# PV in pairs of sequences and heads, selection by four products, and later gathers, in a one-core attention and FFN kernel

## What is computed

```python
xc = einsum('bct,bcd->bdt', x, cond_weights[subject])   # a 32x32 matrix of 32, chosen per sequence
q, k, v = rope(xc @ wq.T), rope(xc @ wk.T), xc @ wv.T   # 32 heads of 16
p = softmax(causal(q @ k.T) / 4)                        # 32x32 per head and sequence
x = x + (p @ v) @ wo.T
h = x @ W.T + 2 * lora(x)        # 8 experts of rank 16, the two best by a router
x = x + unperm(down @ gelu(up @ perm(h)))   # 16 blocks of 32 features, 128 wide inside
```

## Time and profile before

| | |
|---|---|
| median of 3 runs | 212.55 us (211.69 to 213.61) |
| the profiled execution, its own time | 214.02 us |
| its span, first to last instruction | 212.2 us |
| mean granted TensorE clock | 0.984 |
| PE busy | 203.5 us, 96% of the span |
| ACT busy | 119.2 us, 56% |
| DVE busy | 148.0 us, 70% |
| the chain that ended last | PE 89%, DVE 4%, ACT 3%, issue 1%, DMA 1% |

### The profile page before, as it was taken

How to read it: one execution, slowest core, us unless ns; L and a number is a source line. 1 busy time by engine, 2 the same in 40 slices (tenths; PEclk the granted TensorE clock), 3 DMA queues, 4 the chain that set the end, 5 groups by cost and what they waited for, 6 DMA issues and landing times.

```text
span 212.2 us, 6020 instructions
## 1 busy us (share of the span) xinstructions
PE 203.5 (96%) x2548; PEld 176.2 (83%) x2548; DVE 148.0 (70%) x287; ACT 119.2 (56%) x209; POOL 119.2 (56%) x93
## 2 busy tenths in 40 slices
PE   7799999999989999999999999999999999798993
PEld 5699987988769899986779899886698987688863
DVE  4897799999749877837619788546678995258123
ACT  2491465279763445289744454399755777533460
POOL 8263999699770203978982113969978253524000
PEclk9859999999999999999999999999999999999999
DMA  6999602005001330000062420000135200224002
GB/s 198 383 395 375 206 3 103 0 5 197 3 5 47 102 99 3 2 5 0 0 67 38 123 78 3 0 3 2 12 41 127 26 3 3 24 28 49 0 3 99
DMA packets 9930, 15.18 MB, mean 72 GB/s; under 512 B 1328, under 2 KB 5680, under 8 KB 9904
## 3 DMA queue, kind: packets, MB, share of 16 engines
q1 hardware_dynamic: 7440, 11.37, 15.6%
q0 software_dynamic: 2048, 2.88, 8.4%
q10 hardware_dynamic: 416, 0.55, 0.8%
HBM read 11.13 MB, written 3.67 MB: 70 GB/s over the span
## 4 chain that ended last, share of the span: by engine, by line
PE 89%; DVE 4%; ACT 3%; issue 1%; DMA 1%; ACTq 0%; DVEq 0%
PE ps_A L624 11%; PE ps_F L624 10%; PE ps_A L626 10%; PE ps_A L625 10%; PE ps_F L625 9%; PE ps_F L626 9%; PE ps_S L778 5%; PE ps_F L868 5%; PE ps_S L883 3%; PE ps_S L756 3%; PE ps_A L681 2%; PE ps_A L778 1%; PE ps_A L896 1%; ACT pbd L1056 1%; DMA y<-in_ids 1%
## 5 line engine op out<-in xcount | busy, mean ns | idle before, releaser
L570 POOL TENSOR_TENSOR pr<-pr,small 128x512 f32<-128x512 f32 x16 | 17.6, 1110 | 38.8 <-DVE small L1419 38.6
L1056 ACT ACTIVATE pbd<-pr 32x512 f32<-32x512 f32 x56 | 35.2, 629 | 1.3 <-DVE pr L1425 0.6
L550 POOL DMA_INDIRECT out<-y,row_at x12 | 19.8, 1647 | 11.4 <-ACT y L1056 8.9
L1117 ACT ACTIVATE pr<-pr 128x512 f32<-128x512 f32 x16 | 10.1, 633 | 24.4 <-DVE pr L1411 24.3
L507 POOL TENSOR_TENSOR rot<-rot,cst 128x512 f32<-128x512 f32 x11 | 14.4, 1305 | 15.9 <-DVE rot L1377 15.9
L1161 ACT ACTIVATE act<-ps_F 128x512 f32<-128x512 f32 x32 | 16.5, 603 | 11.3 <-PE ps_F L868 11.3
L1397 DVE TENSOR_TENSOR kbd<-kr,cst 128x512 f32<-128x512 f32 x13 | 18.9, 1486 | 3.0 <-POOL kr L511 3.0
L520 POOL TENSOR_TENSOR kbd<-kr,cst 128x512 f32<-128x512 f32 x15 | 19.4, 1320 | 0.1
L624 PE MATMUL ps_F<-x,w2T 128*128 128x256 f32 x56 | 16.1, 287 | 0.0
L626 PE MATMUL ps_F<-x,w2T 128*128 128x256 f32 x56 | 15.6, 279 | 0.0
L625 PE MATMUL ps_F<-x,w2T 128*128 128x256 f32 x56 | 15.6, 279 | 0.0
(11 more groups left out here) (237 smaller groups left out, 662.8 us busy)
## 6 DMA issues: line engine op xcount, KB each, us to landing
xt<-in_xT SPq DMA_DIRECT2D x4, 512.0 KB, 4.1
xs<-in_x SPq DMA_DIRECT2D x3, 512.0 KB, 8.0
out<-xt SPq DMA_DIRECT2D x3, 512.0 KB, 3.1
act<-in_L_attn_wk SPq DMA_DIRECT2D x1, 1024.0 KB
act<-in_L_attn_wv SPq DMA_DIRECT2D x1, 1024.0 KB
act<-in_L_attn_wo SPq DMA_DIRECT2D x1, 1024.0 KB, 7.1
xs<-in_x ACTq DMA_DIRECT2D x1, 512.0 KB, 5.1
pr<-in_L_attn_wq SPq DMA_DIRECT2D x2, 256.0 KB, 4.8
```

The lines of the kernel that those rows point to most:

```text
L550: pool.indirect_dma_start(out=out, out_offset=bass.IndirectOffsetOnAxis(ap=row_at[:, g, c:c + 1], axis=0), in_=y[:, c, :], in_offset=None, ...
L570: pool.tensor_tensor(pr[:, i, :, :], pr[:, i, :, :], mx[:, i, :].unsqueeze(2).to_broadcast([P, NH // 2, T]), ALU.mult).then_inc(normed, 1)
L1056: return sc.activation(dst, src, ACT.Copy)
```

## The change

- `vz` becomes, for each head pair, two slots (s = 0, 1, the sequences 0 and 1, or 2 and 3 of the tile) of 32 columns. Rows 0 to 63 hold the two sequences of the pair with head k = 0, rows 64 to 127 the same two with head k = 1, each with zeros in the other head's columns. `v_out` does this in 4 copies of 64 rows x 256.
- `pbd` becomes, for each head pair and s, 64 columns: two sequences' 32 tokens. Its rows are (head, sequence of the pair, key). `probs_block` does it in 8 copies of 32 rows x 256 in place of 4 of 32 x 512. The last tile's `probs_half` likewise: 4 copies for each half on VectorE and 4 on GpSimd, in place of 2 and 2.
- `pv` has still 8 products, of 64 moving columns instead of 128, and none accumulates.
- The one-hot matrix has zeros outside its own 32 rows (by `matrix_at`, which comes with the indices, and no longer waits for the constants), so 4 products with 128 rows of contraction select all, and one transpose replaces four.
- GpSimd no longer zeroes `pbd`: ScalarE copies zeros from `vz` into it (4 copies of 128 x 512), behind its `blocks(1)`. `kbd_zeros` clears half as much.
- x of group 0 is issued by SP behind the constants and ahead of `wq`.
- GpSimd's gathers wait for `wk` rather than for the last of `wq`.
- `idle_products` 6 and 4 become 5 and 3.

```diff
-        wsel = sb("wsel", [P, T, T])
+        wsel = sb("wsel", [P, SC, BT, TILES])
-        vz = sb("vz", [P, 3, NH // 2, 3 * HD])
+        vz = sb("vz", [P, 3, NH // 2, 2, 2 * HD])
-        pbd = sb("pbd", [P, 2, NH // 2, BT, T])
+        pbd = sb("pbd", [P, 2, HC, 2, 2 * T])
+        def pairs_of(tile, b, k):
+            rows = P // 2 * k + T * (b % 2)
+            return tile[rows:rows + T, :, b // 2, T * (b % 2):T * (b % 2) + T]
+        def heads_of(turned_half, b, k):
+            return turned_half[T * b:T * b + T, :, :].rearrange("p (q k) t -> p q k t", k=2)[:, :, k, :]
...
             sp.dma_start(cst[:, 0:EARLY], consts[:, 0:EARLY]).then_inc(d_cst, 16)
+            load_x(0)
...
-            for i in range(2):
-                pool.memset(pbd[:, i, :, :, :], 0.0).then_inc(pbd_zero, 1)
             pool.wait_ge(d_ids, 16)
-            pool.wait_ge(d_wq2, 16)
+            pool.wait_ge(d_w["wk"], 16)
             perm_rows()
...
-                    last = pe.matmul(bank(it)[at, 0:SC * T], onehot[rows, at], wst[rows, :],
+                    last = pe.matmul(bank(it)[at, 0:SC * T], onehot[:, at], wst[:, :],
                                      start=True, stop=True, skip_group_check=True)
...
-                for e in range(2):
+                for s in range(2):
+                    at = P * c + P // 2 * s
                     for j in range(4):
-                        last = pe.matmul(bank(it)[32 * j:32 * j + 32, P * c:P * c + P],
-                                         vz_of(g, t)[:, 4 * c + j, HD * e:HD * e + 2 * HD],
-                                         pbd_of(g, t, c // 2)[:, HC * (c % 2) + 2 * j + e, :, :],
-                                         start=(e == 0), stop=(e == 1), skip_group_check=True)
+                        last = pe.matmul(bank(it)[32 * j:32 * j + 32, at:at + P // 2], vz_of(g, t)[:, 4 * c + j, s, :],
+                                         pbd_of(g, t, c // 2)[:, HC // 2 * (c % 2) + j, s, :],
+                                         start=True, stop=True, skip_group_check=True)
...
-            idle_products(6, rings["S"][0])
+            idle_products(5, rings["S"][0])
+            pe.wait_ge(d_cst, 16)
             pe.wait_ge(onehot_ready, 1)
-            for r in range(BT):
-                select(r)
-            idle_products(4, rings["S"][0])
+            select()
+            idle_products(3, rings["S"][0])
...
-                dst = vz_of(g, t).rearrange("p q (s f) -> p q s f", f=HD)[:, :, 0:3:2, :]
-                copy(dst, bank(it)[:, :].rearrange("p (q s f) -> p q s f", s=2, f=HD)).then_inc(s_free(it), 1)
+                heads = bank(it)[:, :].rearrange("p (q k f) -> p q k f", k=2, f=HD)
+                for s in range(2):
+                    for k in range(2):
+                        last = copy(vz_of(g, t)[P // 2 * k:P // 2 * k + P // 2, :, s, HD * k:HD * k + HD],
+                                    heads[P // 2 * s:P // 2 * s + P // 2, :, k, :])
+                last.then_inc(s_free(it), 1)
...
                 for b in range(BT):
-                    at = slice(T * b, T * b + T)
-                    last = copy(pbd_of(g, t, i)[at, :, b, :], pT(2 * t + i)[at, :, :])
+                    for k in range(2):
+                        last = copy(pairs_of(pbd_of(g, t, i), b, k), heads_of(pT(2 * t + i), b, k))
                 last.then_inc(pbd_a, 1)
...
             sc.dma_start(ids, who).then_inc(d_ids, 16)
-            sc.dma_start(xs[:, 0, :, :], x_d[0]).then_inc(d_x[0], 16)
...
             blocks(1)
+            sc.wait_ge(vz_zero, 1)
+            for i in range(2):
+                for h in range(2):
+                    copy(pbd[:, i, HC // 2 * h:HC // 2 * h + HC // 2, :, :].rearrange("p q s k -> p (q s k)"),
+                         vz[:, 0, 0:HC, :, :].rearrange("p q s f -> p (q s f)")).then_inc(pbd_zero, 1)
...
-            for r in range(BT):
-                turn_selected(r)
+            turn_selected()
```

More of the change, by code:

```diff
@@ L155, in ropes_to @@
             return 4 * g + i if g else min(i + 1, 3)
-        kbd_pbd = [kbd[:, i, :, :, :].rearrange("p c b k -> p (c b k)").rearrange("p (h b t) -> p h b t", b=BT, t=T)
-                   for i in range(2)]
+        kbd_pbd = [kbd[:, i, :, :, :].rearrange("p c b k -> p (c b k)")[:, 0:HC * 4 * T].rearrange(
+            "p (q s k) -> p q s k", q=HC, s=2) for i in range(2)]
         def pbd_of(g, t, i):
@@ L253, in f_fill @@
                 F_AT[name] = len(F_AT)
-        f_fill(*(("sel", r) for r in range(BT)), ("Q", 0), ("Q", 1), ("K", 0), ("K", 1), ("scores", 0),
+        f_fill(("sel",), ("Q", 0), ("Q", 1), ("K", 0), ("K", 1), ("scores", 0),
                ("scores", 1))
@@ L493, in _ @@
         def _(pool):
-            pool.memset(vz[:, 0:2, :, :], 0.0).then_inc(vz_zero, 1)
+            pool.memset(vz[:, 0:2, :, :, :], 0.0).then_inc(vz_zero, 1)
             def perm_rows():
@@ L528, in kbd_zeros @@
                 wait_full(pool, S_scores(G - 1, 2 * t + 1))
-                pool.memset(kbd[:, t, :, :, :], 0.0).then_inc(kbd_zero, 1)
+                pool.memset(kbd_pbd[t], 0.0).then_inc(kbd_zero, 1)
             def wo_half(h):
@@ L540, in third_v @@
                 wait_full(pool, prep("w2", KC - 1))
-                pool.memset(vz[:, 2, :, :], 0.0).then_inc(vz_zero, 1)
+                pool.memset(vz[:, 2, :, :, :], 0.0).then_inc(vz_zero, 1)
             def add_rows(g, *cs):
@@ L1074, in blocks @@
                 for b in range(2):
-                    i = sc.activation(wbd[:, :, b, :], wsel_of(g), ACT.Copy,
+                    i = sc.activation(wbd[:, :, b, :].rearrange("p t (r d) -> p t r d", r=BT), wsel_of(g), ACT.Copy,
                                       scale=con("pair")[:, b:b + 1])
@@ L1143, in probs_block @@
                 else:
-                    sc.wait_ge(pbd_zero, 2)
+                    sc.wait_ge(pbd_zero, 4)
                 for b in range(BT):
-                    at = slice(T * b, T * b + T)
-                    last = copy(pbd_of(g, t, i)[at, :, b, :], pT(2 * t + i)[at, :, :])
+                    for k in range(2):
+                        last = copy(pairs_of(pbd_of(g, t, i), b, k), heads_of(pT(2 * t + i), b, k))
                 last.then_inc(pbd_a, 1)
@@ L1345, in first_cond_lo, with turn_selected @@
                                  ).then_inc(s_free(it), 1)
-            def turn_selected(r):
-                it = Fi("sel", r)
+            def turn_selected():
+                it = Fi("sel")
                 wait_full(ve, it)
-                ve.transpose(wsel[:, SC * r:SC * r + SC, :].rearrange("p d t -> p (d t)"),
+                ve.transpose(wsel[:, :, :, :].rearrange("p d r t -> p (d r t)"),
                              bank(it)[:, 0:SC * T]).then_inc(s_free(it), 1)
             def blocks(g):
-                for r in range(BT):
-                    wait_read(ve, Fi("sel", r))
+                wait_read(ve, Fi("sel"))
                 if g:
@@ L1431, in probs_half @@
                 for b in range(2):
-                    at = slice(T * b, T * b + T)
-                    last = ve.tensor_copy(pbd_of(G - 1, 1, i)[at, :, b, :], pT(2 + i)[at, :, :])
+                    for k in range(2):
+                        last = ve.tensor_copy(pairs_of(pbd_of(G - 1, 1, i), b, k), heads_of(pT(2 + i), b, k))
                 last.then_inc(pbd_v, 1)
```

44 lines of the change are left out of this document (25 added, 19 removed).

## The result

The changed kernel takes 229.74 us (median, 227.59 to 231.51), the kernel before 212.61 beside it: a ratio of 1.0723, 95% interval 1.0634 to 1.0813. It is slower, as forecast, but by 15.4 us (by the ratio; 17.1 between the medians) and not by 6, and outside the range (209.5 to 223.5). Executions more than 1.5% above the fastest of the same kernel count in the medians and not in the ratios.

The account below looks back on a forecast made before the run. PE's work was taken to set the time from 60 to 178 us, with ACT's margin 0.1 us. Start -2.0, group 0 +3.2, groups 1 and 2 +2.6 each, last group -0.4 gave +6.0: 218.5 us, range 209.5 to 223.5.

Parts of the forecast that it names:

- The copies on ACT: ACT's new copies do not overlap: a block's eight take 3.4 us against 2.56 (+0.88), `v_out` 1.57 (+0.97).
- Group 0: Three longer blocks from 43.77 us on and the longer `v_out` on ACT delay PE's `cond(2)` by 3.2 us.
- group 1: ACT's last `probs_block` comes late for PV's second half on PE, so `cond(3)` starts 2.6 us later.
- group 2: Same order of work as group 1, so the same delay from ACT's late copies: +2.6 us.
- last group: ACT's longer blocks stay hidden and most of PE's gain runs into waits for GELU: -0.4 us (0 to -1.8).
- PV on PE: A half tile with 64 columns takes 0.55 us, a gain of 0.45; at most 7.2 us over 16 half tiles.
- Rival D: PV on PE gets no shorter, which adds about 1.5 us: 220 us; chance 0.05.
- A: ACT's new copies overlap by 0.09 us as the `kbd` copies do: 209.5 to 210.5 us; chance 0.29.
- B: Half of ACT's new copies overlap, a block takes 3.0 us (+0.45), sum +1.4: 214 us; chance 0.16.
- The start: Before group 0's chain: `wbd` ready earlier, `first_conds` near 5.6 us instead of 7.96, worth -2.0 us (-1.0 to -2.6).
- rival C: PE's clock falls in the new gaps of 3.4 us, up to 3.35 us each: 222 to 228 us; chance 0.12.

## Why the direction was right and the size wrong

**The copies on ACT: right.** Eight in 3.38 to 3.41 us (forecast 3.4), `v_out` 1.55 (1.57). Group 0 +3.3 (+3.2), group 1 +2.6 (+2.6), group 2 +2.4 once the clock is taken off (+2.6), last group -0.7 (-0.4), although PE waits 1.5 us there for GpSimd's copies, which I had 0.1 to 0.3 late. The one wait of 3.4 us forecast before PV's second half came in three parts in group 1 (0.90 before the second half of the tile before, 0.81 and 2.52 before the two halves of this one), with the same end. Splitting the copies in the kernel before, and nothing else, costs 6.0 us by places.

**PV on PE: right, a little high.** From its start to the next product's, a half tile takes 0.59 us where 0.55 was forecast, and took 1.01: it gains 0.42 where it stands alone (0.45), and 0.31 where two follow each other (1.86 us for both, then 1.24). Rival D, no shorter PV, is wrong.

**Rivals A and B: wrong, and now for a shown reason.** The overlap needs the same rows in and out. The rule of the Trainium skill, page ScalarE: Activation LUTs, section What ACT_TABLE_LOAD costs, that back-to-back ACTIVATEs overlap by about 93 ns, holds here for copies on the same rows (0.13 us) and not for these. What set `kbd` and `pbd` apart in the trace was the right thing to go by, and A, at 0.29, had more than it deserved.

**The start: the term of -2.0 was +0.5.** The first step held: `first_conds` began at 6.00 (forecast 5.6) with no half clock behind it, and the kernel before with the new start reached the scores of the second tile at 33.78, 1.3 us earlier. But that gain is the spared half clock, and the old start is spared part or all of it in some executions. The kernel before with eight copies, whose start is the old one, reached these scores at 33.48, with half clock over 10 to 14 us only (0.57). The kernel before with the new PV, whose start is the old one but for a `pbd` half as large to clear, had full clock there (1.00 over 9 to 16 us, behind a wait of 1.14) and reached them earlier than any profile with the new start:

```profile
32.69 0.39 PE L757 MATMUL ps_S<-mask_b,ident_b 32*128 32x512 bf16 x2 [1.46 <-DVE xc L1353]
```

At a mean clock of 1.00 the kernel before took 210.4 and 210.6 us on the chip of these runs, the one with the new start 210.5 to 211.2. So the -2.0 was counted from an execution with the fall in it, and at equal clock the runs show no gain by the new start. Two things took back what the spared fall gave. The gathers were costed at 1.4 us each from near 11 us, over by 17 us; they began at 12.21 and took 6.9 us, to 19.14, and that moves the scores to 34.65 in the kernel with the hold. The rest, 0.9 us to 35.55, fits the new PV: `v_out` of the first tiles, 1.0 us longer each, stands on ACT right before the copy of xc that releases these scores; the first is hidden in ACT's wait of 2.45 us for `kr`, the second is not. This is read from the timeline and no run isolates it; in the profiles of the two other held kernels with the new PV the same scores came at 36.16 and 36.38, so executions differ there by as much. ACT's timeline in the changed kernel:

```profile
25.46 1.54 ACT L1065 ACTIVATE vz<-ps_A 64x256 f32<-64x256 f32 x4
29.44 2.45 ACT L1103 ACTIVATE kbd<-kr,cst 128x128 f32<-128x128 f32 x8 [2.45 <-POOL kr L522]
31.91 1.55 ACT L1065 ACTIVATE vz<-ps_A 64x256 f32<-64x256 f32 x4
33.49 1.09 ACT L1094 ACTIVATE xc<-ps_S 128x512 fp32r<-128x512 f32 x2
```

The chain of group 0 was costed from 43.77 on, and the two `v_out` ahead of that were not priced at all.

**The clock: the step that failed.** The sum has no term for the clock: full clock in the new gaps was taken as given, and the fall left to rival C. It measured 5.5 us in the profiled execution, more than any other term was off. C had the mechanism and nearly the price: 222 to 228 with one to three falls, and the profile has three. It was given 0.12, on the strength of one place in the last group where PE did nothing for 1 us and the clock stayed. That was weak evidence against it: at the start a gap of 1.49 us was followed by half clock, and the new gaps were forecast at 2 to 3.4 us, three of them. And the fall was given a small chance, where it comes in each of the timed executions of the changed kernel (mean clock 0.94 to 0.97). With C's chance at half or more, the forecast would have been 222 to 228, whose upper end is still 1.7 us short of the 229.74; the start's missing 2.5 us are more than that.

**What stays open.** Which waits make the clock fall. Length alone does not decide it: behind a wait of 0.7 us before `cond(2)` the clock was full in the kernel before and fell in the one with the new start; behind 1.53 us before the scores of the second tile it fell in one kernel with filled waits and not in the other. In the changed kernel the wait of 2.52 us at 115.94 was followed by full clock; the kernel with early gathers had as long a wait there and then half clock over 113 to 122 us. The mean clock of one kernel's executions differs from run to run (0.94 to 0.97), so the same waits do not always have the same end. That the falls behind the new waits hang on those waits is shown by the fills; the point from which a wait brings one about is not.

## What to carry to other kernels

A copy onto a block diagonal costs more, the more instructions it is cut into (3.40 us in eight, 2.54 in four): halve the columns of a product by doubling the copies that feed it only if the engine that copies has the time before PE asks, block by block, not on the average. Where a forecast makes new gaps of some 2 us in a PE that was full, count the fall of its clock as likely, as it came here behind most of them, and price it beside each gap. Before crediting a change with a spared fall, look whether the kernel before has it in every execution. When a transfer's issue is held back, count what stands behind it on the same engine by when the last issue ends, not the first.

## What the runs showed of the hardware

- Four copies of 32 x 512 on ACT took 2.17 us on the same rows, and 2.55 as soon as the rows read or the rows written changed from one to the next.
- Half clock came behind waits of PE of 0.7 to 2.7 us, and not behind every one: 2.52 us were followed by full clock once. In the profiles of four kernels it cost `cond(2)` 1.3 to 1.7 us in its 32 products alone (3.26 to 3.68 for 2.00). Filling products in the waits removed it there, and 6.2 us with it (5.5 by the ratios).
- Four gathers on GpSimd took 6.9 us in all four profiles in which they were held until `wk` had landed, and 5.3 to 5.6 us when issued earlier, with one of 6.5 (0.95 to 1.99 us each). The Trainium skill, page SBUF — State Buffer, section Who interferes with whom, has GpSimd's writing of descriptors starved of its port by copies and casts of VectorE that use both port pairs. In the changed kernel VectorE's casts ran from 14.66 to 15.58, beside the second gather (1.93 us); beside the third (1.99) ran no copy or cast, but products and a shuffle. No run here takes them away, so that this is the cause is not shown.
- The same page has a copy of VectorE that uses both its port pairs and an instruction of GpSimd lock each other out. Four copies of 32 x 256 took 4.14 us beside four GpSimd products (56.53 to 60.78 us), against 1.91 and 1.90 in groups 1 and 2, where these products had ended within 0.6 us of the copies' start. No run takes the products away, so the cause is not shown; the difference is.
- VectorE's multiplication for the biases (128 x 64) took 1.49 us beside GpSimd's memset of `pbd`, ending 0.05 us after it, and 0.19 us in the changed kernel, which has no such memset (forecast: 1.1 us less).
